# An attention block whose softmax is formed on turned scores: maximum from k's high part, exponential after the turn, one scaling per pair of heads

## The chip, the cores and the metric

The kernel runs on one core of a Trainium2 chip. The metric is the device time of one execution in microseconds (us); less is better. The median of three runs of the kernel before is 2279.28 us (2278.8 to 2279.79).

## What is computed

```python
scale_shift = emb @ W_emb + b_emb                       # 8 x 2048
xn = rms_norm(x, g_norm) * (1 + scale) + shift          # x: 8 x 512 x 1024, float32
q, k, v = split(xn @ W_qkv)                             # 16 heads of 64
q, k = rms_norm(q, g_q), rms_norm(k, g_k)
attn = softmax(q @ k.T * 64 ** -0.5)                    # 512 x 512 for each head and batch
o = attn @ v
return x + o + o @ W_out
```

Everything is float32. The kernel gets that accuracy from TensorE's one-pass float32r products by splitting each operand into a high part, rounded to float32r, and a low part, the rest: a product is then high by high, high by low and low by high.

## The kernel before, in words

**Tiling.** The work goes batch by batch (8 batches of 512 tokens, 4 token tiles of 128), and within a batch by pairs of heads (8 pairs; `it` = batch * 8 + pair counts 64 of them). Each engine has a written list of steps for the first batch (HEAD), the six in the middle (BODY) and the last (TAIL). A step is named by the pair, a letter and a number: `5S2` is step S, number 2, of pair 5; pairs 8 and 9 are the first two of the next batch, which run ahead. The engines go through their lists in order, and semaphores between them hold a step until its input is there. A step that waits holds everything behind it on its engine.

**The steps of TensorE.** C: a quarter of one token tile of the product with W_qkv, 6 matmuls of 384 columns into `proj_bank` (two banks in turn); P the same for W_out. T: 4 transposes of q (T0) or k (T1) into `flip_bank`. S: scores of head n // 4 and query tile n % 4, into `score_bank` (two in turn). F: turns the probabilities of 128 keys by all 512 queries, 4 transposes of 128 x 128 into `flip_bank` (two in turn, shared by T, F and X, which turns x). W: the product of v with the turned probabilities, two matmuls of 512 columns (high and low part of the probabilities) into `pv_bank`.

**The steps beside it.** For a projected tile: ScalarE's D copies v and squares q and k, VectorE's D sums the squares, GpSimd's D adds epsilon and raises to the power of -1/2, VectorE's M scales q and k and so frees the bank. T: ScalarE writes the high parts, VectorE the low parts. `q_split[head]` holds q's high part in the head's 64 rows and its low part in the other 64; `k_hi[head]` holds k's high part twice, so one matmul over 128 contraction rows gives (q high + q low) by k high; `k_lo[head]` has k's low part in the head's rows and zeros in the others.

For a score tile: VectorE's S takes the row maximum (negated) from PSUM; ScalarE's S takes the exponential with that as bias into `probs` and accumulates the row sum; VectorE's N takes the reciprocal of the row sum and scales the tile in place. After F: ScalarE's F copies the turned tile, rounded, to `pt_hi`, VectorE's F subtracts that from the turned tile in PSUM into `pt_lo`. O joins the two halves of `pv_bank` (ScalarE moves one to the other rows, VectorE adds), Q splits the result into `o_hi` (ScalarE) and `o_lo` (GpSimd). V splits v, L and Y split weights and x, R adds the residual, A and X normalize the next batch's x. SyncE issues the DMAs for weights, x, residual and results.

The lines concerned: TensorE's S is lines 585 to 592, F 593 to 600, W 601 to 611; ScalarE's S 714 to 720, F 721 to 724; VectorE's S 857 to 860, N 861 to 866, F 867 to 870, O 871 to 877; GpSimd's D 968 to 974.

Of the kernel before, what the change touches and what calls it, by code (L numbers as in the profile page):

```python
# [36 lines left out]
        1C5 1C6 1C7 1C8 1C9 0S0 0S1 1C10 1C11 0S2 0S3 1C12 1C13 0S4 0S5 1C14 0F0 0F1 1C15 0S6 0S7 2C0 0F2 0F3 0W0 0W1  # L37
        2C1 2C2 0W2 2C3 0W3 1T0 1T1 2C4 2C5 2C6 2C7 0F4 2C8 2C9 0F5 1S0 0F6 0W4 1S1 2C10 0F7 0W5 1S2 1S3 0W6 2C11 0W7
        2C12 1S4 1S5 1F0 1F1 2C13 2C14 1F2 1W0 1F3 1W1 1S6 1S7 1W2 2C15 1W3 3C0 3C1 1F4 1F5 3C2 3C3 2T0 2T1 1W4 1W5 3C4
        3C5 3C6 1F6 3C7 3C8 1F7 1W6 2S0 2S1 3C9 3C10 1W7 2S2 3C11 3C12 2S3 2S4 3C13 3C14 3C15 2S5 2S6 4C0 2F0 2F1 4C1  # L40
        4C2 2S7 4C3 3T0 3T1 2W0 2W1 4C4 4C5 2F2 4C6 4C7 4C8 2F3 2W2 3S0 2F4 3S1 2F5 2W3 4C9 3S2 2F6 2W4 3S3 2F7 2W5 4C10
        2W6 4C11 2W7 3S4 3S5 4C12 3F0 3F1 4C13 3S6 4C14 3F2 3W0 3F3 3W1 3S7 4C15 3W2 5C0 3W3 3F4 3F5 5C1 5C2 3F6 3F7 3W4
        3W5 5C3 5C4 4T0 4T1 3W6 3W7 5C5 5C6 5C7 5C8 5C9 4S0 4S1 5C10 5C11 4S2 4S3 5C12 5C13 4S4 4S5 5C14 4F0 4F1 5C15
        4S6 4S7 6C0 4F2 4F3 4W0 4W1 6C1 6C2 5T0 4W2 5T1 4W3 6C3 6C4 6C5 4F4 6C6 6C7 6C8 4F5 5S0 4F6 4W4 5S1 6C9 4F7 4W5
        4W6 5S2 6C10 4W7 5S3 6C11 5S4 6C12 5S5 5F0 5F1 6C13 6C14 5F2 5W0 5F3 5W1 5S6 5S7 5W2 6C15 5W3 7C0 7C1 5F4 5F5
        7C2 7C3 +X0 5W4 5W5 7C4 6T0 7C5 6T1 7C6 7C7 7C8 7C9 5F6 7C10 7C11 +X1 5W6 6S0 6S1 5F7 7C12 7C13 7C14 7C15 +X2
        5W7 6S2 6S3 8C0 8C1 +X3 8C2 6S4 6S5 8C3 8C4 6S6 8C5 7T0 6S7 8C6 7T1 8C7 8C8 8C9 6F0 8C10 8C11 6F1 6F2 6W0 7S0
        7S1 6F3 6W1 6F4 6W2 8C12 7S2 6F5 6W3 7S3 6F6 6W4 8C13 6F7 6W5 7S4 6W6 8C14 8C15 6W7 7S5 7F0 7F1 7S6 9C0 9C1 7F2
# [1102 lines left out]
```

## Time and profile before

| | |
|---|---|
| median of the runs | 2279.28 us |
| the profiled execution | 2278.89 us, its span 2276.0 us |
| TensorE, matmuls | 2256.2 us busy (99%), 13392 matmuls |
| VectorE | 1597.9 us (70%) |
| ScalarE | 1345.7 us (59%) |
| GpSimd | 651.7 us (29%) |

The span is from the first to the last instruction of the profiled execution. A matmul's end is modelled and matmuls overlap in the pipeline, so the distance between the starts of two matmuls says more than the duration of one. Durations of VectorE and ScalarE overlap slightly with their neighbours too.

### The profile page before, as it was taken

To read this page: it belongs to the slowest core of one execution; us is meant where nothing else is said; L and a number is where in the kernel's file an instruction comes from. 1 tells how busy PE (TensorE), PEld (TensorE's weight loads), DVE (VectorE), ACT (ScalarE), POOL (GpSimd) and SP (SyncE) were. 2 spreads that over 40 slices of the span, in tenths; PEclk is the share of its full clock that TensorE was granted. 3 is DMA by queue.
4 is the path that set the end of the run, shared out by engine and by line. 5 is a ranking of instruction groups with operands and counts; after the bars stand their busy time and mean duration, and the time that the engine had idled before them with its cause. 6 is when DMAs were issued, how large, how long until landed. Compare 5 with 4: busy or idle time off the path is not lost.

```text
span 2276.0 us, 36733 instructions
## 1 busy us (share of the span) xinstructions
PE 2256.2 (99%) x13392; PEld 2110.3 (93%) x13392; DVE 1597.9 (70%) x3284; ACT 1345.7 (59%) x3101; POOL 651.7 (29%) x880
## 2 busy tenths in 40 slices
PE   8999999999999999999999999999999999999999
PEld 4999989999999999999999999999999999999999
DVE  4898784787827778287872878738786487854875
ACT  4687772667616676176762667526674366743663
POOL 3444431324213241122312234122331223302220
PEclk9999999999999999999999999999999999999999
DMA  9544346422364332733236332362323723246331
GB/s 359 224 167 177 112 154 228 178 99 110 118 220 184 107 115 88 256 148 112 111 114 256 112 112 112 122 253 107 112 112 130 291 92 118 82 151 246 111 121 65
DMA packets 71269, 346.35 MB, mean 152 GB/s; under 512 B 7601, under 2 KB 43441, under 8 KB 47537
## 3 DMA queue, kind: packets, MB, share of 16 engines
q1 hardware_dynamic: 71088, 344.01, 41.2%
q8 instruction: 106, 1.74, 0.3%
q14 instruction: 75, 0.61, 0.1%
HBM read 293.65 MB, written 50.33 MB: 151 GB/s over the span
## 4 chain that ended last, share of the span: by engine, by line
PE 86%; DVE 8%; ACT 2%; issue 1%; POOL 0%; DMA 0%; ACTq 0%; DVEq 0%
PE proj_bank L502 18%; PE proj_bank L500 18%; PE proj_bank L501 18%; PE flip_bank L598 9%; PE pv_bank L609 5%; PE pv_bank L610 5%; PE score_bank L590 4%; PE score_bank L591 4%; PE flip_bank L553 2%; DVE probs L865 2%; DVE neg_max L859 2%; DVE pt_lo L869 2%; PE flip_bank L563 1%; ACT k_hi L700 1%; PE proj_bank L525 1%
## 5 line engine op out<-in xcount | busy, mean ns | idle before, releaser
L500 PE MATMUL proj_bank<-w_split,xn_hi 128*128 128x384 f32 x2048 | 700.0, 342 | 1.4 <-DVE res L907 0.8
L502 PE MATMUL proj_bank<-w_split,xn_lo 128*128 128x384 f32 x2048 | 688.5, 336 | 0.0
L501 PE MATMUL proj_bank<-w_split,xn_hi 128*128 128x384 f32 x2048 | 687.4, 336 | 0.0
L718 ACT ACTIVATE probs<-score_bank,neg_max 128x512 f32<-128x512 f32 x512 | 352.6, 691 | 213.5 <-DVE neg_max L859 211.2
L500 PEld LDWEIGHTS proj_bank<-w_split,xn_hi 128*128 128x128 f32 x2048 | 385.2, 188 | 18.1 <-DVE xn_lo L854 1.0
L501 PEld LDWEIGHTS proj_bank<-w_split,xn_hi 128*128 128x128 f32 x2048 | 385.5, 188 | 15.2
L724 ACT CAST pt_hi<-flip_bank 128x512 fp32r<-128x512 f32 x512 | 288.8, 591 | 182.0 <-PE flip_bank L598 91.1
L869 DVE TENSOR_TENSOR pt_lo<-flip_bank,pt_hi 128x512 fp32r<-128x512 f32 x512 | 339.9, 685 | 78.1 <-ACT pt_hi L724 75.9
L502 PEld LDWEIGHTS proj_bank<-w_split,xn_lo 128*128 128x128 f32 x2048 | 384.8, 188 | 0.0
L859 DVE TENSOR_REDUCE neg_max<-score_bank 128x1 f32<-128x512 f32 x512 | 341.3, 684 | 17.0 <-PE score_bank L591 13.0
L865 DVE TENSOR_SCALAR probs<-probs,row_inv 128x512 f32<-128x512 f32 x512 | 275.7, 539 | 18.1
L598 PE MATMUL flip_bank<-ident,probs 128*128 128x128 f32 x2048 | 284.4, 273 | 1.1 <-DVE q_split L830 0.4
L598 PEld LDWEIGHTS flip_bank<-ident,probs 128*128 128x128 f32 x2048 | 242.5, 140 | 32.8 <-DVE pt_lo L869 7.3
L973 POOL TENSOR_TENSOR qk_rstd<-qk_ms_eps,neg_half 128x4 f32<-128x4 f32 x256 | 264.6, 1033 | 20.0
L970 POOL TENSOR_TENSOR qk_ms_eps<-qk_ms,eps_col 128x4 f32<-128x4 f32 x256 | 55.3, 216 | 719.2 <-DVE qk_ms L880 719.1
L609 PE MATMUL pv_bank<-pt_hi,v_split 128*128 128x512 f32 x512 | 224.3, 438 | 4.2 <-DVE pt_lo L869 4.2
L500 PE MATMUL proj_bank<-w_split,o_hi 128*128 128x384 f32 (+1 forms) x672 | 215.2, 320 | 0.0
L951 POOL TENSOR_TENSOR v_split<-v_stage,v_split 128x256 fp32r<-128x256 f32 x128 | 98.9, 773 | 401.3 <-ACT v_split L688 401.3
L502 PE MATMUL proj_bank<-w_split,o_lo 128*128 128x384 f32 (+1 forms) x672 | 213.6, 318 | 0.0
L501 PE MATMUL proj_bank<-w_split,o_hi 128*128 128x384 f32 (+1 forms) x672 | 213.5, 318 | 0.0
L590 PE MATMUL score_bank<-k_hi,q_split 128*128 128x512 f32 x512 | 206.0, 402 | 0.1
L591 PE MATMUL score_bank<-k_lo,q_split 128*128 128x512 f32 x512 | 201.6, 394 | 0.0
(86 smaller groups left out, 3205.1 us busy)
## 6 DMA issues: line engine op xcount, KB each, us to landing
w_split<-w_store SPq DMA_DIRECT2D x140, 1536.0 KB, 7.0
w_store<-w_split SPq DMA_DIRECT2D x20, 1536.0 KB, 10.1
x_tile<-in_x SPq DMA_DIRECT2D x32, 512.0 KB, 11.0
w_raw<-in_w_qkv SPq DMA_DIRECT2D x16, 768.0 KB, 8.4
w_split<-w_store SPq DMA_DIRECT2D x12, 1024.0 KB, 5.1
w_raw<-in_x SPq DMA_DIRECT2D x56, 192.0 KB, 6.7
out<-w_raw SPq DMA_DIRECT2D x56, 192.0 KB, 1.9
emb_stage<-in_w_emb SPq DMA_DIRECT2D x5, 1024.0 KB, 10.6
```

The lines of the kernel that those rows point to most:

```text
L500: nc.tensor.matmul(dst, a_hi, w_hi, start=(kt == 0), stop=False)
L501: nc.tensor.matmul(dst, a_hi, w_lo, start=False, stop=False)
L502: mm = nc.tensor.matmul(dst, a_lo, w_hi, start=False, stop=(kt == KT - 1))
L590: nc.tensor.matmul(score_bank[n % 2][:, :], q_t, k_hi[h][:, :], start=True, stop=False)
L591: nc.tensor.matmul(score_bank[n % 2][:, :], q_t, k_lo[h][:, :], start=False, stop=True).then_inc(score_full, 1)
L598: mm = nc.tensor.transpose(flip_bank[flip][:, qt * P:(qt + 1) * P], probs[h][:, qt, i * P:(i + 1) * P], ident[:, :])
L609: nc.tensor.matmul(pv_bank[h][:, :], v_t, pt_hi[n % 2][:, :], start=(i == 0), stop=False)
L718: nc.scalar.activation(probs[h][:, i, :], score_bank[n % 2][:, :], ACT.Exp, bias=neg_max[:, n:n + 1], accum_out=row_sum[:, n:n + 1]).then_ ...
L724: nc.scalar.copy(pt_hi[n % 2][:, :], flip_bank[flip][:, :]).then_inc(flip_hi, 1)
L859: nc.vector.tensor_reduce(neg_max[:, n:n + 1], score_bank[n % 2][:, :], AX.X, ALU.max, negate=True).then_inc(max_done, 1)
L865: nc.vector.tensor_scalar(probs[h][:, i, :], probs[h][:, i, :], row_inv[:, n:n + 1], None, ALU.mult).then_inc(probs_ready, 1)
L869: nc.vector.tensor_tensor(pt_lo[n % 2][:, :], flip_bank[flip][:, :], f32(pt_hi[n % 2][:, :]), ALU.subtract).then_inc(flip_free, 1)
```

## The change

Step S of TensorE is one matmul, with `k_hi` alone, and serves for the maximum only. Step H (new) turns the four columns of negated maxima of a head into four rows of 128; VectorE's H lays them, by a product with the identity, as four rows of 512 over a copy of q (`q_max`, made by VectorE's Z) where `k_lo` has four rows of ones. Step F then forms the scores a second time, already turned, in two matmuls of 512 columns: `k_hi` by `q_split`, and `k_lo` by `q_max`, whose four extra contraction rows add the negated maximum. ScalarE's F takes the exponential of the turned scores into `probs`; its new step E copies that, rounded, to `pt_hi`; VectorE's F takes `pt_lo` from `probs` and `pt_hi`, both in SBUF. The probabilities stay unscaled. Their sums over the keys are formed by GpSimd's new step U (six adds of 128 x 512 a pair), ScalarE's U and VectorE's N (the two heads brought into one tile), J (high and low part) and TensorE's G, two matmuls with a matrix of ones per head. VectorE's G takes the reciprocal of the 128 x 512 sums and scales `o_pair` once. The flip banks are handed back by two semaphores, one for each engine that frees them. `o_part` and one of the three first residual buffers go. The orders of all engines but SyncE are written anew; shown are the lines of BODY that hold the steps of pair 5's scores (TensorE before; TensorE, VectorE and GpSimd after).

```diff
-        4C4 3T0 3T1 2W2 2W3 4C5 4C6 4C7 2F4 4C8 4C9 2F5 3S0 2F6 2W4 3S1 4C10 2F7 2W5 3S2 3S3 2W6 4C11 2W7 4C12 3S4 3S5
-        5C7 5C8 3F7 3W6 4S0 4S1 5C9 3W7 5C10 4S2 4S3 5C11 5C12 4S4 5C13 4S5 5C14 4F0 4F1 4S6 4S7 5C15 4F2 4F3 4W0 4W1
...
+        4H1 5C14 4W0 4F3 4F4 4W1 5C15 4F5 4F6 4W2 4W3 4F7 6C0 6C1 4W4 4W5 5T0 5T1 6C2 4W6 4W7 6C3 6C4 6C5 5S0 5S1 6C6
+        6C7 6C8 4G0 5S2 6C9 5S3 6C10 6C11 5H0 5S4 5S5 6C12 5F0 5F1 5S6 5S7 6C13 5F2 5F3 6C14 5H1 5W0 5W1 6C15 5F4 5F5
...
+        4N0 4N1 4O1 6M0 4J0 6D1 5S0 5S1 4G0 6M1 5S2 5S3 5H0 6D2 5S4 5S5 6M2 5S6 5S7 5F0 5F1 5H1 5F2 5F3 6D3 5F4 5F5 6M3
...
+        3U0 3U1 4D3 3U2 3U3 3U4 3U5 5D0 4V0 4V1 5D1 3Q0 5D2 4U0 4U1 5D3 4U2 4U3 5V0 4U4 4U5 6D0 5V1 6D1 4Q0 6D2 5U0 5U1
...
-        q_split = [sb(f"q_split{h}", [P, T], F32R) for h in range(2)]
+        q_split = sb("q_split", [P, 2, T], F32R)
+        q_max = sb("q_max", [P, 2, T], F32R)
...
-                        pe.wait_ge(exp_done, it * 8 + (n - 2 + 1 + CREDIT))
+                        wait_past(pe, max_done, it * 8 + (n - 1))
                         if n == 0:
-                            pe.wait_ge(flip_free, flip_at(order, b, "T", 1, p)[0] + 1)
-                        q_t = q_split[h][:, i * P:(i + 1) * P]
-                        nc.tensor.matmul(score_bank[n % 2][:, :], q_t, k_hi[h][:, :], start=True, stop=False)
-                        nc.tensor.matmul(score_bank[n % 2][:, :], q_t, k_lo[h][:, :], start=False,
-                                         stop=True).then_inc(score_full, 1)
+                            pe.wait_ge(qk_hi_done, it * 2 + 2)
+                            freed(pe, "T", 0, it)
+                        nc.tensor.matmul(score_bank[n % 2][:, :], q_split[:, h, i * P:(i + 1) * P], k_hi[h][:, :],
+                                         start=True, stop=True).then_inc(score_full, 1)
+                    elif kind == "H":
+                        flip_wait(pe, u)
+                        pe.wait_ge(max_done, it * 8 + 4 * n + 4)
+                        nc.tensor.transpose(flip_bank[flip][0:TT, 0:P], neg_max[:, 4 * n:4 * n + 4],
+                                            ident[:, :]).then_inc(flip_full, 1)
                     elif kind == "F":
-                        wait_past(pe, flip_free, releases(order, u))
+                        flip_wait(pe, u)
                         if i == 0:
-                            pe.wait_ge(probs_ready, it * 8 + (4 * h + 4))
-                        for qt in range(TT):
-                            mm = nc.tensor.transpose(flip_bank[flip][:, qt * P:(qt + 1) * P],
-                                                     probs[h][:, qt, i * P:(i + 1) * P], ident[:, :])
-                        mm.then_inc(flip_full, 1)
+                            freed(pe, "H", h, it)
+                            freed(pe, "T", 1, it)
+                        nc.tensor.matmul(flip_bank[flip][:, :], k_hi[h][:, i * P:(i + 1) * P], q_split[:, h, :],
+                                         start=True, stop=False)
+                        nc.tensor.matmul(flip_bank[flip][:, :], k_lo[h][:, i * P:(i + 1) * P], q_max[:, h, :],
+                                         start=False, stop=True).then_inc(flip_full, 1)
...
+                    elif kind == "G":
+                        flip_wait(pe, u)
+                        if is_first(it):
+                            pe.wait_ge(ones_ready, 2)
+                        pe.wait_ge(sum_lo_done, it + 1)
+                        nc.tensor.matmul(flip_bank[flip][:, :], head_ones[:, :], sum_hi, start=True, stop=False)
+                        nc.tensor.matmul(flip_bank[flip][:, :], head_ones[:, :], sum_lo, start=False,
+                                         stop=True).then_inc(flip_full, 1)
...
-                    elif kind == "S":
-                        act.wait_ge(max_done, it * 8 + (n + 1))
-                        if i == 0 and not (is_first(b) and p == 0):
-                            act.wait_ge(flip_full, flip_at(order, b, "F", 4 * h + 3, p - 1)[0] + 1)
-                        nc.scalar.activation(probs[h][:, i, :], score_bank[n % 2][:, :], ACT.Exp,
-                                             bias=neg_max[:, n:n + 1],
-                                             accum_out=row_sum[:, n:n + 1]).then_inc(exp_done, 1)
                     elif kind == "F":
                         act.wait_ge(flip_full, u + 1)
+                        if i == 0 and not is_first(it):
+                            if h == 0:
+                                act.wait_ge(key_sum_done, it * 2 - 1)
+                            else:
+                                freed(act, "G", 0, it - 1)
+                        nc.scalar.activation(probs[h][:, i, :], flip_bank[flip][:, :],
+                                             ACT.Exp).then_inc(flip_freed["ScalarE"], 1)
+                    elif kind == "E":
                         act.wait_ge(pv_used, it * 8 + (n - 1 + CREDIT))
-                        nc.scalar.copy(pt_hi[n % 2][:, :], flip_bank[flip][:, :]).then_inc(flip_hi, 1)
+                        owner, done = RELEASES[flip_of("F", n, it)]
+                        act.wait_ge(flip_freed[owner], done)
+                        nc.scalar.copy(pt_hi[n % 2][:, :], probs[h][:, i, :]).then_inc(p_hi_done, 1)
+                    elif kind == "U":
+                        mine, other = rows(n), rows(1 - n)
+                        act.wait_ge(keys_added, it * 6 + (5 if n == 0 else 6))
+                        nc.scalar.copy(key_moved[mine, :], probs[n][other, 3, :]).then_inc(keys_moved, 1)
+                    elif kind == "J":
+                        act.wait_ge(key_sum_done, it * 2 + 2)
+                        nc.scalar.copy(sum_hi, key_sum).then_inc(sum_hi_done, 1)
...
+                    elif kind == "Z":
+                        freed(dve, "T", 0, it)
+                        nc.vector.tensor_copy(q_max[:, :, :], f32(q_split[:, :, :])).then_inc(q_copied, 1)
...
+                    elif kind == "H":
+                        dve.wait_ge(flip_full, u + 1)
+                        dve.wait_ge(q_copied, it + 1)
+                        at = (1 - n) * DH
+                        nc.vector.tensor_tensor(q_max[at:at + TT, n, :].rearrange("p (t q) -> p t q", q=P),
+                                                flip_bank[flip][0:TT, 0:P].unsqueeze(1).to_broadcast([TT, TT, P]),
+                                                ident[0:TT, 0:TT].unsqueeze(2).to_broadcast([TT, TT, P]),
+                                                ALU.mult).then_inc(flip_freed["VectorE"], 1)
+                    elif kind == "F":
+                        dve.wait_ge(p_hi_done, it * 8 + (n + 1))
+                        nc.vector.tensor_tensor(pt_lo[n % 2][:, :], probs[h][:, i, :], f32(pt_hi[n % 2][:, :]),
+                                                ALU.subtract).then_inc(p_lo_done, 1)
                     elif kind == "N":
-                        dve.wait_ge(exp_done, it * 8 + (n + 1 + CREDIT))
-                        nc.vector.reciprocal(row_inv[:, n:n + 1], row_sum[:, n:n + 1]).then_inc(inv_done, 1)
-                        dve.wait_ge(inv_done, it * 8 + (n + 1))
-                        nc.vector.tensor_scalar(probs[h][:, i, :], probs[h][:, i, :], row_inv[:, n:n + 1], None,
-                                                ALU.mult).then_inc(probs_ready, 1)
-                    elif kind == "F":
-                        dve.wait_ge(flip_hi, u_hi + 1)
-                        nc.vector.tensor_tensor(pt_lo[n % 2][:, :], flip_bank[flip][:, :],
-                                                f32(pt_hi[n % 2][:, :]), ALU.subtract).then_inc(flip_free, 1)
+                        mine = rows(n)
+                        dve.wait_ge(keys_moved, it * 2 + (n + 1))
+                        nc.vector.tensor_tensor(key_sum[mine, :], probs[n][mine, 3, :], key_moved[mine, :],
+                                                ALU.add).then_inc(key_sum_done, 1)
+                    elif kind == "J":
+                        dve.wait_ge(sum_hi_done, it + 1)
+                        nc.vector.tensor_tensor(sum_lo, key_sum, f32(sum_hi), ALU.subtract).then_inc(sum_lo_done, 1)
+                    elif kind == "G":
+                        dve.wait_ge(flip_full, u + 1)
+                        dve.wait_ge(sum_lo_done, it + 1)
+                        dve.wait_ge(o_sum_done, it * 2 + (2 + CREDIT))
+                        nc.vector.reciprocal(sum_inv, flip_bank[flip][:, :]).then_inc(inv_done, 1)
+                        dve.wait_ge(inv_done, it + 1)
+                        nc.vector.tensor_tensor(o_pair[:, :], o_pair[:, :], sum_inv,
+                                                ALU.mult).then_inc(flip_freed["VectorE"], 1)
                     elif kind == "O":
                         dve.wait_ge(o_part_done, it * 2 + (n + 1))
-                        if n == 0:
-                            dve.wait_ge(o_lo_done, it + 1)
                         mine = rows(n)
-                        nc.vector.tensor_tensor(o_pair[mine, :], pv_bank[n][mine, :], o_part[mine, :],
+                        nc.vector.tensor_tensor(o_pair[mine, :], pv_bank[n][mine, :], o_pair[mine, :],
                                                 ALU.add).then_inc(o_sum_done, 1)
...
+            def add_keys(it, n):
+
+                head, part = n // 3, n % 3
+                e = probs[head]
+                if part < 2:
+                    pool.wait_ge(p_lo_done, it * 8 + (4 * head + 2 * part + 2))
+                    src, dst = 2 * part, 2 * part + 1
+                else:
+                    pool.wait_ge(keys_added, it * 6 + n)
+                    src, dst = 1, 3
+                op = nc.gpsimd.tensor_tensor(e[:, dst, :], e[:, src, :], e[:, dst, :], ALU.add)
+                op.then_inc(keys_added, 1)
 
```

## Rows read from the trace of the kernel before

**Rows 1.** The page, parts 1 and 2: busy time, and the granted clock by slices.

```profile
PE 2256.2 (99%) x13392; PEld 2110.3 (93%) x13392; DVE 1597.9 (70%) x3284; ACT 1345.7 (59%) x3101; POOL 651.7 (29%) x880
...
PEclk9999999999999999999999999999999999999999
```

**Rows 2.** The page, part 4: the chain that ended last, by engine.

```profile
PE 86%; DVE 8%; ACT 2%; issue 1%; POOL 0%; DMA 0%; ACTq 0%; DVEq 0%
```

**Rows 3.** The waits: who waited for whom, us in total, times, longest.

```profile
PE pv_bank L609 <- DVE pt_lo L869: 4.2, 7, 0.6
```

**Rows 4.** The timeline of TensorE: start, duration, line, operands, count.

```profile
700.28 0.40 PE L590 MATMUL score_bank<-k_hi,q_split 128*128 128x512 f32 x1
700.52 0.39 PE L591 MATMUL score_bank<-k_lo,q_split 128*128 128x512 f32 x1
700.74 0.34 PE L500 MATMUL proj_bank<-w_split,xn_hi 128*128 128x384 f32 x1
...
701.79 1.03 PE L598 MATMUL flip_bank<-ident,probs 128*128 128x128 f32 x8
702.58 0.42 PE L500 MATMUL proj_bank<-w_split,xn_hi 128*128 128x384 f32 x1
702.84 0.34 PE L501 MATMUL proj_bank<-w_split,xn_hi 128*128 128x384 f32 x1
```

**Rows 5.** Groups of TensorE by line and form: busy, mean ns, idle before.

```profile
L598 PE MATMUL flip_bank<-ident,probs 128*128 128x128 f32 x2048 | 284.4, 273 | 1.1 <-DVE q_split L830 0.4
```

**Rows 6.** The same view for VectorE.

```profile
L859 DVE TENSOR_REDUCE neg_max<-score_bank 128x1 f32<-128x512 f32 x512 | 341.3, 684 | 17.0 <-PE score_bank L591 13.0
L869 DVE TENSOR_TENSOR pt_lo<-flip_bank,pt_hi 128x512 fp32r<-128x512 f32 x512 | 339.9, 685 | 78.1 <-ACT pt_hi L724 75.9
L865 DVE TENSOR_SCALAR probs<-probs,row_inv 128x512 f32<-128x512 f32 x512 | 275.7, 539 | 18.1
...
L880 DVE TENSOR_REDUCE qk_ms<-sq 128x4 f32<-128x256 f32 x256 | 106.1, 414 | 86.2 <-ACT sq L742 83.6
...
L863 DVE RECIPROCAL row_inv<-row_sum 128x1 f32<-128x1 f32 x512 | 80.7, 158 | 55.1 <-ACT probs L718 54.0
...
L918 DVE TENSOR_SCALAR gq_col<-gq_raw 128x1 f32<-128x1 f32 x1 | 0.1, 147 | 0.0
```

**Rows 7.** The same view for ScalarE.

```profile
L718 ACT ACTIVATE probs<-score_bank,neg_max 128x512 f32<-128x512 f32 x512 | 352.6, 691 | 213.5 <-DVE neg_max L859 211.2
L724 ACT CAST pt_hi<-flip_bank 128x512 fp32r<-128x512 f32 x512 | 288.8, 591 | 182.0 <-PE flip_bank L598 91.1 <-PE pv_bank L610 88.6
...
L718 ACT ACTIVATION_READ_ACCUMULATOR probs<-score_bank,neg_max 128x1 f32 x512 | 102.3, 200 | 0.0
L742 ACT ACTIVATE sq<-proj_bank 128x256 f32<-128x256 f32 x256 | 100.5, 393 | 0.0
```

**Rows 8.** The same view for GpSimd.

```profile
L973 POOL TENSOR_TENSOR qk_rstd<-qk_ms_eps,neg_half 128x4 f32<-128x4 f32 x256 | 264.6, 1033 | 20.0
...
L966 POOL TENSOR_TENSOR o_lo<-o_pair,o_hi 128x512 fp32r<-128x512 f32 x64 | 84.3, 1317 | 381.1 <-ACT o_hi L734 380.9
```

**Rows 9.** The timeline of VectorE in the first batch.

```profile
40.78 0.69 DVE L854 TENSOR_TENSOR xn_lo<-y_half,xn_hi 128x512 fp32r<-128x512 f32 x1 [0.30 <-ACT xn_hi L666]
...
42.85 3.79 DVE L767 TENSOR_TENSOR w_split<-w_raw,w_split 128x384 fp32r<-128x384 f32 x3
...
49.72 0.55 DVE L767 TENSOR_TENSOR w_split<-w_raw,w_split 128x384 fp32r<-128x384 f32 x1
```

**Rows 10.** The timeline of GpSimd in the same stretch.

```profile
42.64 2.29 POOL L933 TENSOR_TENSOR w_split<-w_raw,w_split 128x384 fp32r<-128x384 f32 x2
```

**Rows 11.** The timeline of all engines around 297 us.

```profile
297.56 1.57 POOL L966 TENSOR_TENSOR o_lo<-o_pair,o_hi 128x512 fp32r<-128x512 f32 x1
...
298.65 0.66 PE L553 MATMUL flip_bank<-ident,qk_stage 128*128 128x128 f32 x4 [1.48 <-DVE pt_lo L869]
```

**Rows 12.** Busy time of each engine in a dense stretch: us, count, clock, DMA.

```profile
850.00:900.00 50.00, 49.91 (x294) 46.25 (x293) 41.70 (x83) 33.82 (x76) 11.44 (x16) 1.00 0.30 110
```

More of the change, by code:

```diff
@@ L226, in flip_buf, with order_of, flip_table @@
-def flip_buf(order, kind, n, p):
-    places = HEAD_FLIPS if order is HEAD else TAIL_FLIPS if order is TAIL else BODY_FLIPS
-    before = 0 if order is HEAD else HEAD_FLIPS[1]
-    assert BODY_FLIPS[1] % 2 == 0
-    return (before + places[0][(kind, n, p)][0]) % 2
-FIRST_X = {HEAD_FLIPS[0][("X", r, 0)][0] for r in range(TT)}
-def releases(order, u):
-    return u if order is HEAD and u - 2 in FIRST_X else u - 1
+def order_of(b):
+    return HEAD if b == 0 else TAIL if b == B - 1 else BODY
+def flip_table():
+    table, releases, counts = {}, [], {"ScalarE": 0, "VectorE": 0}
+    for b in range(B):
+        for step in order_of(b)["TensorE"]:
+            p, d, kind, n = read_step(step)
+            if kind in "TFXHG":
+                table[(kind, n, b + d if kind == "X" else b * PAIRS + p)] = len(releases)
+                for owner in ("VectorE", "ScalarE") if kind == "X" else ("ScalarE",) if kind == "F" else ("VectorE",):
+                    counts[owner] += 1
+                    releases.append((owner, counts[owner]))
+    return table, releases
@@ L337, in cond_attention @@
         v_split = [sb(f"v_split{h}", [P, TT, P], F32R) for h in range(2)]
-        probs = [sb(f"probs{h}", [P, TT, T]) for h in range(2)]
+        probs = [sb("probs0", [P, TT, T])]
+        with nc.sbuf_tensor("sum_split", [P, TT, T], F32R) as sum_split:
+            pass
+        probs.append(sb("probs1", [P, TT, T]))
         pt_hi = [sb(f"pt_hi{i}", [P, T], F32R) for i in range(2)]
@@ L557, in cycle @@
                         for half in range(2):
-                            wait_past(pe, flip_free, releases(order, u + half))
+                            flip_wait(pe, u + half)
                             if half == 0:
@@ L911, in _ @@
             for head in range(2):
-                nc.vector.memset(f32(k_lo[head][rows(1 - head), :]), 0.0)
+                op = nc.vector.memset(f32(k_lo[head][rows(1 - head), :]), 0.0)
+            op.then_inc(k_lo_zero, 1)
+            dve.wait_ge(k_lo_zero, 1)
+            for head in range(2):
+                nc.vector.memset(f32(k_lo[head][(1 - head) * DH:(1 - head) * DH + TT, :]), 1.0)
             for kt in range(0, KT, 2):
```

383 lines of the change are left out of this document (198 added, 185 removed).

## The prediction

> **What bounds the kernel now.** I read the page first: TensorE is busy for 2256.2 of 2276.0 us and its granted clock stands at nine tenths or more in all forty slices, the upper level of 2.4 GHz [rows 1]. Busy ends are modelled, so I went to the chain of waits: 86% of it is TensorE, 8% VectorE [rows 2], and the table of waits, where the largest wait of a matmul in the attention is 4.2 us in all [rows 3]. Then the timeline of TensorE alone, for its true prices, which are the distances between starts: 0.46 us for two matmuls of 512 columns (0.230 each, against 0.40 of "duration"), 1.05 us for one C step of six matmuls of 384 columns, and 0.79 us for 8 transposes after which the next matmul comes 0.26 instead of 0.17 us later, so 0.875 per 8, 0.109 each [rows 4]. The reader should see there that nothing waits: every matmul starts when the one before it has been fed. So the time is TensorE's list of instructions, plus some waits. The steps of its three orders, counted from the code and priced so, sum to 2201 us; the other 75 us of the span (the start before the first batch, and small waits) I leave as they are. In a dense stretch VectorE is busy for 41.7 of 50 us, 83% [rows 12]: the next bound is near.
>
> **TensorE, the terms.** There are 64 pairs (8 batches by 8), 8 tiles each.
> - F loses its transposes: 2048 of them [rows 5] by 0.109 = 224.0 us.
> - S loses its second matmul: 512 by 0.230 = 117.8 us.
> - F gains two matmuls of 512 columns: 1024 by 0.230 = 235.5 us.
> - G: 2 matmuls by 64 by 0.230 = 29.4 us.
> - H: 2 single transposes a pair. The trace has none alone; 0.055 (half of one, since only 4 weight columns are loaded) and 0.2 (one plus the later start of the next matmul) bound it. I take 0.109, the row's mean: 14.0 us, ends 7 and 26.
> Net: 224.0 + 117.8 - 235.5 - 29.4 - 14.0 = 62.9 us less, all of it on the path, since TensorE is it. By H's ends, 51 to 70.
>
> **What now has to hide.** ScalarE: the exponential stays (691 ns, now from the turned scores and without bias), its 8 reads of the accumulator (200 ns) go, the copy to pt_hi stays at about its 591 ns [rows 7]; U twice and J once are three such copies, 1.8 us for 1.6 us gone. Neutral, at 60% busy. One wait gets shorter: a score bank is free after the maximum alone, and a flip bank after the exponential alone.
> VectorE, by a pair: gone are 8 scalings at 539 ns and 8 reciprocals at 158, 5.6 us. New are Z (1024 columns, between 0.66 and 1.4; by the scaling's 539 for 512, about 1.0), H twice, N twice, J and G's product, six instructions at about 685 each [rows 6], 4.1 us, and G's reciprocal of 512 columns. By the slope of the row reductions, 684 against 414 ns for 256 columns more [rows 6], VectorE goes at 1.05 ns an element, so 0.69. Sum 5.8: no change, if two things hold, and both become rivals below.
> GpSimd: U, 6 adds of 512 columns a pair, at o_lo's 1317 ns [rows 8]: 7.9 us a pair, 506 us in all, on top of 652. It isn't full (52%), but its queue also holds D, whose power takes 1033 ns and ends in the release of a projection bank. The order has D behind one or two U steps (4U0 4U1 5D3), so M3 comes up to 1.3 us later; four C steps (4.2 us) stand between two uses of a bank, against a chain of 0.3 + 0.4 + 0.4 + 0.2 + 1.0 + 0.4 = 2.7 us, so 1.3 us fits but not 2.6.
>
> **The walk where it is tightest.** In BODY, TensorE from the end of 5S1: 6C6 6C7 6C8 (3.15), 4G0 (0.46), 5S2 (0.23), 6C9 (1.05), 5S3 (0.23), 6C10 6C11 (2.10): 5H0 is reached at 7.22 us. VectorE has 6D1 before 5S0, and 6D1's tile ends with 6C7 at 2.10; ScalarE's copy and square take some 0.66 (the square 393 ns [rows 7], the copy of half as many columns 0.27 by estimate), 6D1 ends at 3.2, then 5S0 5S1 4G0 6M1 5S2 5S3 at 0.68 + 0.68 + 1.38 + 0.42 + 0.68 + 0.68: 7.7 by durations, some 7.2 if each starts 0.1 us before its forerunner's end, as rows in sequence do. So 5H0 has no slack, and everything dearer on VectorE between 5S0 and 5H0 is a wait of TensorE, once a pair. In the same way 5H0 to 5F0 is 1.5 us, against about 1.0 for VectorE's H and its semaphores: fits. From F to its W stand 3.3 to 6.4 us, against 0.69 + 0.6 + 0.69 and some 0.3 for the semaphores = 2.3: at least 1.0 to spare. W7 to the next G is 5.7 us or more; O, N, J lie in it.
>
> **The shared port.** The rows of VectorE with two inputs from SBUF: 0.55 us for 384 columns and 0.69 for 512 alone, but three of 384 columns in 3.79 us, 1.26 each [rows 9], while GpSimd ran two of its own in 2.29 us [rows 10]. And it has reached TensorE once: around 297 us GpSimd's o_lo took 1.57 instead of 1.32, and a transpose waited for VectorE's pt_lo, 1.48 us idle [rows 11]. Before, pt_lo took one input from PSUM and never met this (685 mean, [rows 6]); now all 8 pt_lo a pair have both in SBUF, as have N, J and G's product, and GpSimd's SBUF work grows from about 3 to 11 us a pair, some 0.4 of a dense pair's 27 us. An instruction that arrives in a GpSimd add waits for 0.65 on the mean: 12 by 0.4 by 0.65 = 3 us of VectorE's time a pair. Most of it falls in the F stretch, where ScalarE's 1.3 us for each F sets the pace and the 1.0 us above covers it. I take 0.4 us a pair as what gets through to TensorE, 25 us; the ends are 0 and 3 us a pair.
> The Trainium skill, SBUF — State Buffer, Who interferes with whom, says that a VectorE instruction with two SBUF inputs contends with a GpSimd instruction that reads SBUF, and that the later one waits for the whole of the earlier; [rows 9, 10] agree (1.26 against 0.55). By that rule the worst single wait is one add, 1.3 us.
>
> **Sum.** From the profiled execution (span 2276.0, whole time 2278.9, which is 0.4 under the median of the three runs): 2278.9 - 62.9 + 25 = 2241 us. Its own range: 2208 (no new wait, H at its low end) to 2265.
>
> **Rival A, the reciprocal becomes the wait (slower).** The trace has the reciprocal of one column only: 158 ns against 147 for a scaling of one column [rows 6]. Those 11 ns bound it from above at 1 + 11, or 12 ns an element, 6 us for 512; from below it is 0.69. If the divider takes 8 turns an element at 1.05 ns, G's reciprocal is 512 by 8.4 = 4.3 us, 3.6 more than I put in, and by the walk nearly all of it becomes a wait of TensorE before H0, in some 60 of 64 pairs: 3.3 by 60 = 200 us, so 2440. Half of that speed gives 2330. It decides from 1.0 us a pair over my price, a reciprocal of 1.7 us. For it: only the one-column row. Against it: the reductions, at two lengths, go at 1.05 ns an element, and 11 ns lie within the spread of such short rows. I put 0.17 on it.
> The Trainium skill, VectorE: DVE Perf Modes, First, the fixed hardware budget, says the reciprocal is an iterative divide with a repeat count of 8; that speaks for this rival, and no row here can show its rate over many columns.
>
> **Rival B, the port eats the gain.** If 1 us of the 3 a pair reaches TensorE, because pt_lo, then M and the next S slip together: 64 us, so 2280; at 0.6 us a pair 2254, at 1.5 it is 2312. It decides from 0.98 us a pair. For it: VectorE at 83% in a dense stretch [rows 12] plus 3 us a pair is some 95% of 27 us, and the 1.48 us of [rows 11]. Against: the slack of F to W. Chance 0.17, for 2265 to 2310.
>
> **Chances and range.** Forecast 0.66, A 0.17, B 0.17. A measurement of this kernel can't tell less than about 0.2%, 4.6 us, from nothing. Faster by more: the forecast and half of B, 0.75. Within: 0.04 of B. Slower: A and the rest of B, 0.21. Range 2208 to 2305: that leaves out A and a little at either end.
>
> **What would show it.** Right: TensorE's F groups as two matmuls 0.23 apart; a batch's period near 272 us instead of 278; pt_lo's mean between 0.8 and 1.0 us with single ones at 1.9; U at 1.3 us; waits of TensorE for VectorE's maximum or H under 1 us a pair. Wrong: a RECIPROCAL of 512 columns above 1.7 us with H or S waiting for a maximum behind it (A); VectorE above 90% in the dense stretches and W waiting for pt_lo (B); an F matmul further apart than 0.23 us, which would break the first sum.

## The result, and the profile after

| | median of the runs | ratio to before, 95% |
|---|---|---|
| before | 2279.04 us (2277.61 to 2279.79) | 1 |
| after | 2539.49 us (2537.11 to 2543.43) | 1.1145 (1.1126 to 1.1165) |

The change makes the kernel 260 us slower; forecast was 2241 us, 38 us faster, and the range ended at 2305. The page of the changed kernel, part 1 (span 2539.1 us), answers to [rows 1]:

```profile
PE 2312.5 (91%) x12112; PEld 2057.5 (81%) x12112; DVE 1942.9 (77%) x2777; ACT 1379.0 (54%) x2781; POOL 1227.3 (48%) x1264
```

TensorE has 1280 matmuls fewer, as the change says, and is no longer busy all the time: 91% instead of 99%. VectorE, which was to have the same work, has 345 us more. The groups of VectorE and GpSimd, in the columns of [rows 6, 8], say where:

```profile
L932 DVE RECIPROCAL probs<-flip_bank 128x512 f32<-128x512 f32 x64 | 214.4, 3350 | 1.4 <-PE flip_bank L635 0.4
L918 DVE TENSOR_TENSOR pt_lo<-probs,pt_hi 128x512 fp32r<-128x512 f32 x512 | 421.1, 851 | 134.8 <-ACT pt_hi L754 133.0
L923 DVE TENSOR_TENSOR probs<-probs 64x512 f32<-64x512 f32 x128 | 103.1, 805 | 11.0 <-ACT probs L758 7.8
L1020 POOL TENSOR_TENSOR probs<-probs 128x512 f32<-128x512 f32 x384 | 513.9, 1342 | 424.6 <-DVE pt_lo L918 418.3
```

The first row is G's reciprocal: 3350 ns, not 0.69 us, 170 us more than priced over 64 pairs. pt_lo's mean rose from 685 ns [rows 6] to 851, as expected; U, the last row, takes the 1.3 us of [rows 8]. L923 is N. Z takes 1271 ns (L882) and J 771 (L927). The waits, as in [rows 3] (who waited for whom, us in total, times, longest):

```profile
PE score_bank L602 <- DVE neg_max L906: 45.9, 32, 2.4
PE proj_bank L512 <- DVE qk_stage L949: 39.2, 32, 2.7
PE flip_bank L607 <- DVE neg_max L906: 36.3, 23, 2.5
PE pv_bank L626 <- DVE pt_lo L918: 20.3, 43, 3.5
PE flip_bank L614 <- DVE o_pair L934: 17.8, 11, 2.2
```

Before, the largest of this kind was 4.2 us in all [rows 3]. Now S (L602), H (L607), C (L512) and F (L614) wait for something that VectorE delivers behind the reciprocal; W's wait (L626) is no shorter without it (22.1 us in experiment 1). One such place, near the end, where the rest is quiet; VectorE first, then TensorE (start, duration, line, tiles, count, idle before it and the releaser):

```profile
2487.71 3.35 DVE L932 RECIPROCAL probs<-flip_bank 128x512 f32<-128x512 f32 x1
2491.09 0.69 DVE L934 TENSOR_TENSOR o_pair<-o_pair,probs 128x512 f32<-128x512 f32 x1
2491.70 1.28 DVE L906 TENSOR_REDUCE neg_max<-score_bank 128x1 f32<-128x512 f32 x2
```

```profile
2492.44 0.79 PE L602 MATMUL score_bank<-k_hi,q_split 128*128 128x512 f32 x1 [2.30 <-DVE neg_max L906]
...
2493.35 0.52 PE L538 MATMUL proj_bank<-w_split,o_hi 128*128 128x384 f32 x1
2493.67 0.52 PE L539 MATMUL proj_bank<-w_split,o_lo 128*128 128x384 f32 x1
```

The maximum that frees a score bank stands in VectorE's queue behind 3.35 + 0.69 us, and TensorE stands idle for 2.3 us. The reader should also see what comes behind the wait: P's matmuls start 0.32 us apart instead of 0.175, up to 2494.95. The same stretch by windows (columns after the length: busy us and count of PE, PEld, DVE, ACT, POOL, then the granted clock):

```profile
2490.00:2492.00 2.00, 0.14 (x1) 0.00 (x0) 1.97 (x3) 0.18 (x1) 0.00 (x0) 1.00 0.00 0
2492.00:2495.00 3.00, 2.56 (x8) 2.27 (x9) 2.04 (x4) 0.43 (x1) 1.28 (x1) 0.55 0.00 0
```

After the wait the clock is granted at 0.55, nearly the lower level of 1.2 GHz. Its mean over the span is 0.976 against 0.999 before. Were TensorE busy in all of the time at the lower level, it would have lost 0.024 by 2539 = 61 us there; that is the most it can be.

A dense stretch, in the columns of [rows 12], has VectorE at 95%:

```profile
1250.00:1300.00 50.00, 41.20 (x207) 35.11 (x207) 47.26 (x65) 28.38 (x58) 28.21 (x28) 1.00 0.20 71
```

It is the fullest 50 us of the trace. Nine of its 50 such stretches stand at 90% or more; before it was 1 of 45.

### The profile page after: what moved, and what is told of

It is laid out like the page before. It is cut to its first block and busy times, and to the rows that moved or that the text cites. A ratio compares the mean times of both kernels' runs of the same rounds, so it can differ in the third digit from the quotient of the medians.

```text
span 2539.1 us, 34110 instructions
## 1 busy us (share of the span) xinstructions
PE 2312.5 (91%) x12112; PEld 2057.5 (81%) x12112; DVE 1942.9 (77%) x2777; ACT 1379.0 (54%) x2781; POOL 1227.3 (48%) x1264
## 3 DMA queue, kind: packets, MB, share of 16 engines
q8 instruction: 97, 1.59, 0.3%
## 5 line engine op out<-in xcount | busy, mean ns | idle before, releaser
L512 PE MATMUL proj_bank<-w_split,xn_hi 128*128 128x384 f32 x2048 | 714.4, 349 | 40.0 <-DVE qk_stage L949 39.2
L1020 POOL TENSOR_TENSOR probs<-probs 128x512 f32<-128x512 f32 x384 | 513.9, 1342 | 424.6 <-DVE pt_lo L918 418.3
L513 PE MATMUL proj_bank<-w_split,xn_hi 128*128 128x384 f32 x2048 | 701.9, 343 | 0.0
L918 DVE TENSOR_TENSOR pt_lo<-probs,pt_hi 128x512 fp32r<-128x512 f32 x512 | 421.1, 851 | 134.8 <-ACT pt_hi L754 133.0
L512 PEld LDWEIGHTS proj_bank<-w_split,xn_hi 128*128 128x128 f32 x2048 | 395.2, 193 | 74.1 <-DVE qk_stage L949 52.6
L748 ACT ACTIVATE probs<-flip_bank 128x512 f32<-128x512 f32 x512 | 288.8, 603 | 195.4 <-PE flip_bank L616 189.3
L754 ACT CAST pt_hi<-probs 128x512 fp32r<-128x512 f32 x512 | 299.1, 625 | 89.2 <-PE pv_bank L627 86.7
L1052 POOL TENSOR_TENSOR qk_ms_eps<-qk_ms,eps_col 128x4 f32<-128x4 f32 x256 | 82.1, 321 | 407.0 <-DVE qk_ms L943 407.0
L771 ACT CAST o_hi<-o_pair 128x512 fp32r<-128x512 f32 x64 | 39.6, 619 | 398.3 <-DVE o_pair L934 250.2
L614 PE MATMUL flip_bank<-q_split,k_hi 128*128 128x512 f32 x512 | 209.9, 410 | 46.8 <-DVE o_pair L934 17.8
L602 PE MATMUL score_bank<-k_hi,q_split 128*128 128x512 f32 x512 | 203.8, 441 | 47.2 <-DVE neg_max L906 45.9
L1048 POOL TENSOR_TENSOR o_lo<-o_pair,o_hi 128x512 fp32r<-128x512 f32 x64 | 87.6, 1368 | 325.9 <-ACT o_hi L771 325.9
L626 PE MATMUL pv_bank<-pt_hi,v_split 128*128 128x512 f32 x512 | 213.2, 416 | 21.1 <-DVE pt_lo L918 20.3
L512 PE MATMUL proj_bank<-w_split,o_hi 128*128 128x384 f32 (+1 forms) x672 | 217.4, 323 | 5.3 <-DVE res L970 4.3
L932 DVE RECIPROCAL probs<-flip_bank 128x512 f32<-128x512 f32 x64 | 214.4, 3350 | 1.4 <-PE flip_bank L635 0.4
```

Source lines behind the costliest of these rows:

```text
L512: nc.tensor.matmul(dst, a_hi, w_hi, start=(kt == 0), stop=False)
L513: nc.tensor.matmul(dst, a_hi, w_lo, start=False, stop=False)
L614: nc.tensor.matmul(flip_bank[flip][:, :], k_hi[h][:, i * P:(i + 1) * P], q_split[:, h, :], start=True, stop=False)
L626: nc.tensor.matmul(pv_bank[h][:, :], v_t, pt_hi[n % 2][:, :], start=(i == 0), stop=False)
L748: nc.scalar.activation(probs[h][:, i, :], flip_bank[flip][:, :], ACT.Exp).then_inc(flip_freed["ScalarE"], 1)
L754: nc.scalar.copy(pt_hi[n % 2][:, :], probs[h][:, i, :]).then_inc(p_hi_done, 1)
```

## The experiments

All times are medians; "a pair" is a 64th of the difference. VectorE's busy time is that of part 1 of each page: 1597.9 us before, 1942.9 after. The runs of the kernel before beside them gave 2277.7 to 2278.9 us.

**1. e1_copy: the division taken out of the change.**

```diff
-nc.vector.reciprocal(sum_inv, flip_bank[flip][:, :]).then_inc(inv_done, 1)
+nc.vector.tensor_copy(sum_inv, flip_bank[flip][:, :]).then_inc(inv_done, 1)
```

> The changed kernel with G's reciprocal of 128 x 512 replaced by a plain copy of the same shape (left out: the division, so o is scaled by the sums). Theory R, the reciprocal is the cause: VectorE is 3.35 - 0.6 = 2.7 us a pair shorter, nearly all of it waits of TensorE (64 x 2.7 = 173 us), and most of the 33 stretches at the lower clock go with it: 2300 to 2340 us. Theory P, the shared port is the cause: at most 40 us less, 2500 us.

Measured: 2357.94 us, ratio 1.0348 (1.0332 to 1.0363). 181.5 us less than after, 2.84 a pair, for 2.67 us of VectorE (3350 - 681 ns). S's wait nearly goes, and H's falls to 1.4 us in all:

```profile
PE score_bank L602 <- DVE neg_max L906: 7.7, 9, 1.3
```

The clock went from 0.976 to 0.991, which is up to 40 of those us. So the reciprocal is 70% of the loss, and 79 us of it are something else. With them the time lies 18 us above the range expected.

**2. e2_no_port: GpSimd's adds on 8 columns instead of 512** (most of the sums over the keys is left out).

```diff
-op = nc.gpsimd.tensor_tensor(e[:, dst, :], e[:, src, :], e[:, dst, :], ALU.add)
+op = nc.gpsimd.tensor_tensor(e[:, dst, 0:8], e[:, src, 0:8], e[:, dst, 0:8], ALU.add)
```

> The changed kernel with GpSimd's six adds a pair cut from 512 to 8 columns (left out: most of the sum over the keys). The reciprocal stays. It takes GpSimd's port time away and with it the waits of pt_lo (851 against a median of 692 ns). Theory R: 512 x 0.16 = 82 us of VectorE's time, a part of it on TensorE: 2470 to 2510 us. Theory P: 2330 us or less.

Measured: 2497.57 us, 1.0954 (1.0936 to 1.0973): 42 us less, 0.65 a pair. pt_lo's mean fell from 851 to 727 ns and Z's from 1271 to 698; VectorE is busy for 123 us less (1820.2), a third of which comes through.

**3. e3_both: both edits.**

> Both edits together (left out: the division and most of the sum over keys). Whatever is left over the 2216 us of the span before less 62.9 is neither the reciprocal nor the port. R and P both: 2235 to 2260 us, clock near 1.0. If it stays above 2300, a third cause exists, such as GpSimd's later D or the new chain S, H, F.

Measured: 2292.19 us, 1.0055 (1.004 to 1.007). With the division out of the way the adds cost 2358 - 2292 = 66 us, 1.03 a pair, more than beside it. VectorE is busy for 136 us less than in e1 (1653.0 against 1789.0), 2.1 a pair. The victims of the adds aren't pt_lo alone. Z, with one input from SBUF, is one; e1 first, then e3:

```profile
L882 DVE CAST q_max<-q_split 128x1024 fp32r<-128x1024 f32 x64 | 81.3, 1270 | 1.7
```

```profile
L882 DVE CAST q_max<-q_split 128x1024 fp32r<-128x1024 f32 x64 | 44.7, 698 | 1.7
```

What is left is 32 us over the expected range and still not faster than before: there is a third loss.

**4. e4_half: half of the columns by reciprocal, half by copy.**

```diff
+nc.vector.reciprocal(probs[1][:, 1, 0:256], flip_bank[flip][:, 0:256])
+nc.vector.tensor_copy(probs[1][:, 1, 256:512], flip_bank[flip][:, 256:512]).then_inc(inv_done, 1)
```

> The changed kernel with the reciprocal of 256 columns and a copy of the other 256 (left out: half of the division). VectorE's part is 1.7 + 0.35 us instead of 3.35. If each us of it costs TensorE a us, the time is halfway between the changed kernel and the copy: 2430 us for R. If slack takes up the first microsecond it is nearer to the copy: 2390.

Measured: 2417.98 us (two executions), 1.0609, clock 0.998 and 0.994. The two take 1.75 + 0.36 us:

```profile
L932 DVE RECIPROCAL probs<-flip_bank 128x256 f32<-128x256 f32 x64 | 111.9, 1748 | 1.4 <-PE flip_bank L635 0.4
```

The first 1.42 us of VectorE cost 60 us (0.66 each), the next 1.24 cost 122 (1.5 each). The second half costs more than its own time; it is there that the clock falls, to 0.976. It doesn't simply follow VectorE's load: e1, with less of it, stands at 0.991.

**5. w2_lnexp: a whole version, the reciprocal on ScalarE as exp(-ln x).**

```diff
+nc.scalar.activation(sum_inv, flip_bank[flip][:, :], ACT.Ln).then_inc(ln_done, 1)
+nc.scalar.activation(sum_inv, sum_inv, ACT.Exp, scale=-1.0).then_inc(flip_freed["ScalarE"], 1)
```

> A version meant to be whole: the reciprocal as exp(-ln(sum)) on ScalarE, at the place just before Q or the next F in its order; VectorE's G is the product alone. ScalarE gets 1.2 us and two table loads of 1.28 us a pair. Theory R: as the copy kernel less 0.6 us of VectorE and plus ScalarE's delays before F0's exponential, up to 1 us a pair: 2310 to 2370 us. Theory P: 2500 us.

Measured: 2505.83 us, 1.0996 (1.0975 to 1.1016). A miss: only 34 us of the 181. Each of the two functions loads a table each time (L755 for Ln; L757, for Exp, has a row with the same 64 loads of 1283 ns), and VectorE's product, which kept its place in the order, waits for ScalarE instead:

```profile
L755 ACT ACT_TABLE_LOAD x64 | 82.1, 1283 | 1.1
```

```profile
DVE o_pair L939 <- ACT probs L757: 188.8, 57, 6.0
```

The work left VectorE, the wait stayed in its queue.

**6. e7_memset: e1 with GpSimd kept as busy, but reading nothing** (the division and the sums are left out). Port or queue?

```diff
-op = nc.gpsimd.tensor_tensor(e[:, dst, :], e[:, src, :], e[:, dst, :], ALU.add)
+nc.gpsimd.memset(e[:, src, :], 1.0)
+op = nc.gpsimd.memset(e[:, dst, :], 1.0)
```

> Leaves out: G's division (a copy in its place) and the sums over the keys (GpSimd writes ones, two memsets of 512 columns for each U step, which read nothing from SBUF). Question: e3's gain over e1 (2358 to 2292) came from GpSimd's adds shrinking. Was it the shared port that they held, or the time that they took in GpSimd's queue ahead of the power that frees a projection bank? The two memsets keep the queue about as busy and hold no input from SBUF. Theory, the port: 2285 to 2305, VectorE's pt_lo at 0.73 us mean as in e3 and no pt_lo above 1.0 us. Rival, the queue: 2345 to 2365, pt_lo as short, but waits of C for qk_stage (POOL power late) as in e1. If memset proves much shorter than 0.6 us each the queue is only partly loaded and a fast run tells little; the duration is to be read first.

Measured: 2298.95 us, 1.0092 (1.0077 to 1.0107). The two memsets take 1.05 us together, against 1.34 for the add, pt_lo's mean is 727 ns (729 in e3) and VectorE is busy for 1662.0 us. So of the 66 us 59 come from what GpSimd's adds read, the shared port, and 7 from its queue, with 78% of the add's time kept in it. One sign did not come: some pt_lo still take over 1.0 us, the longest 1803 ns, beside GpSimd's other work (xn_lo, o_lo).

**7. e10_load_elsewhere: e1 and 2.46 us of reciprocals a pair at another place**, behind the pt_lo of tile 7; their output goes nowhere.

> e1 (G's division left out, 2358) with seven extra reciprocals of 32 columns on VectorE in each pair, behind the pt_lo of tile 7, where W has over 1 us to spare; at 6.5 ns an element and some 0.1 us between them about 2.5 us of VectorE a pair. Output of these goes nowhere. Theory A, only the place counts (the walk from 5S0 to 5H0): this place has slack, at most 0.5 us a pair gets through, 2358 to 2390. Theory B, the load counts (VectorE was at 90% of the dense stretches already, so any 2.5 us is paid wherever it stands): 2358 plus 1.3 to 2.5 us by 64, so 2440 to 2520.

Measured: 2449.96 us, 1.0757 (1.0741 to 1.0773): 92 us, 1.44 a pair for seven of these:

```profile
L925 DVE RECIPROCAL scratch<-neg_half 128x32 f32<-128x32 f32 x448 | 157.4, 351 | 13.2
```

That is 58% of the 2.46 us put in. But VectorE's busy time grew by 97 us only (1886.5 against 1789.0), 1.52 a pair: the added work also moved Z and N away from GpSimd's adds (Z takes 738 ns instead of 1270, N 703 instead of 811). Of what VectorE had more to do, 94% is paid. I had expected at most 0.5 us a pair to get through: theory A, as it was put, falls. The run doesn't exclude that there is some spare time, since 2.46 less the 1.0 of the walk is 1.46 as well; place and load aren't told apart by it.

**8. e5_before_load: the kernel before with 2.76 us of reciprocals a pair**, nothing of it left out.

> The kernel before, all its work kept, with five extra reciprocals of 64 columns on VectorE in each pair right after the scaling of tile 0 (a stretch where the next maxima wait behind them); their output goes nowhere. At 6.5 ns an element some 2.6 us a pair. Question: is the price of a long reciprocal a matter of this change's orders, or does the kernel before pay the same? Theory, any kernel here with VectorE at 83% pays most of it: before plus 1.3 to 2.5 us by 64, 2360 to 2440. Rival, the kernel before has the room (its VectorE waits are all short and it has 17% left): under 0.5 us a pair, 2279 to 2310.

Measured: 2443.51 us, 1.0728 (1.071 to 1.0746). 166 us, 2.59 a pair: 94% of it is paid in the kernel before too, a little more than expected. At this place it didn't have the 17% that it seems to have in [rows 12]: the maxima stand behind the added work, which TensorE's rigid order turns into waits (its longest now: S for the exponential, 41.9 us, W for pt_lo, 39.2 us).

**9. e11_no_n: e3 with N's addition as a copy** (the sums are left out altogether).

```diff
-nc.vector.tensor_tensor(key_sum[mine, :], probs[n][mine, 3, :], key_moved[mine, :],
-                        ALU.add).then_inc(key_sum_done, 1)
+nc.vector.tensor_copy(key_sum[mine, :], probs[n][mine, 3, :]).then_inc(key_sum_done, 1)
```

> e3 (division and GpSimd's wide adds left out, 2292) with N's addition of two SBUF tiles replaced by a copy of one of them, so the sum of the keys is left out altogether. Theory: in e3 N still holds the shared port against GpSimd's power (1.45 instead of 1.01 us), which frees a projection bank late, so C waits 1.3 us once a batch and some smaller times: those waits go, 5 to 12 us less, 2280 to 2287, the longest power at 1.01. Rival: the power is late for another reason (its place in VectorE's and GpSimd's orders), 2289 to 2293.

Measured: 2266.48 us, 0.9951 (0.9936 to 0.9966). The expected 5 to 12 us were too few: 25.7 us, for 2 by 0.25 = 0.49 us of VectorE a pair. The wait that I had named does shrink, but not more than by 8 us; e3 first, then e11:

```profile
PE proj_bank L512 <- DVE qk_stage L949: 14.3, 25, 2.0
```

```profile
PE proj_bank L512 <- DVE qk_stage L948: 5.9, 10, 1.6
```

And GpSimd's longest power is still 1460 ns, where I had said 1.01 us. In e3 the longest stand beside N, in e11 beside pt_lo, which has two inputs from SBUF as well; those above 1.1 us fell from 45 to 21. So that mechanism explains a part at most. VectorE is busy for 30 us less (1623.0), and 86% of that is gained, near to the shares of experiments 7 and 8.

**10. w4_eight_columns: a whole version with a reciprocal of 8 columns.** The core (R is a new step of TensorE; N, J and ScalarE's U are gone):

```diff
+for part in range(2 * TT):                          # G: row sums as 128x8
+    mm = nc.tensor.matmul(flip_bank[flip][:, part:part + 1],
+                          probs[part % 2][:, 3, part // 2 * P:(part // 2 + 1) * P],
+                          ones_col[:, :], start=True, stop=True)
+nc.vector.reciprocal(inv8[:, :], flip_bank[flip][:, 0:2 * TT])
+for part in range(2 * TT):                          # R: one row of inverses per query column
+    mm = nc.tensor.matmul(flip_bank[flip][rows(part % 2), part // 2 * P:(part // 2 + 1) * P],
+                          inv8[:, part:part + 1].to_broadcast([P, DH]), ident[:, :],
+                          start=True, stop=True)
```

> A whole version, nothing left out, in which the long reciprocal isn't needed: GpSimd's sums over the tiles stay (U), but G is now eight small fp32 matmuls, each with 128 queries of the summed probabilities as stationary and one column of ones moving, so the row sums come out as 128 by 8; VectorE's reciprocal has 8 columns; a new TensorE step R (eight small matmuls of the inverses spread over 64 columns against the identity) turns them to one row per head, and the product reads them from PSUM. The two additions N, the copies U of ScalarE and J on both engines go. VectorE's load by a pair: N 1.61, J 0.77, reciprocal 3.35 gone, 6.25 by 8 and 0.15, so 0.2, back: 5.5 us less than in the changed kernel. Theory, the load of VectorE and what stands before H is the loss: it should land near e1 (2358), lower by N and J (e11 gave 26 us for 0.49 us a pair), higher by TensorE's extra: R 8 by 0.05 to 0.095 and G 8 by 0.06 to 0.3 less its old 0.46, so 25 to 170 us; forecast 2370, 2320 to 2440. Rival, the loss lies mainly in the port and the clock: above 2450, as half of the orders' waits stay.

Measured: 2428.89 us, 1.0664 (1.0646 to 1.0682): 111 us less than after, inside the range expected and 59 over its middle. The waits for VectorE's maxima have gone (H's are 1.1 us in all) and W's for pt_lo are down to 11.0; TensorE is the bound again, at 98%, with more work:

```profile
PE 2387.3 (98%) x14032; PEld 2173.3 (90%) x14032; DVE 1594.8 (66%) x2585; ACT 1263.9 (52%) x2589; POOL 1179.8 (49%) x1264
```

```profile
L935 DVE RECIPROCAL inv<-flip_bank 128x8 f32<-128x8 f32 x64 | 13.2, 206 | 82.7 <-PE flip_bank L633 82.7
```

Each of the small matmuls in the code, 8 of G and 8 of R a pair, has two records in the trace. By the distances between starts G's 1024 records take 111.6 us (0.109 each) and R's 1024 take 66.4 (0.065 each), 178 us in place of G's 30. Without these 148 us it would stand at about 2281, an estimate that takes them all to be on the path. No version of the runs that computes the whole reference beats the kernel before; e11 is faster only because it leaves work out.

## Why the prediction was wrong

**The step that failed** is the price of one instruction: "VectorE goes at 1.05 ns an element, so 0.69", the slope of the row reductions carried over to G's reciprocal. The runs give five widths: 206 ns for 8 columns, 351 for 32, 551 for 64, 1748 for 256, 3350 for 512, a line of 150 + 6.25 ns a column. The row of one column, 158 ns [rows 6], lies on it too, but one width gives no slope. I set it against a one-column scaling of 147 and got "12 ns an element at most", a factor of 2 too high; the reductions, the row of another operation, were a factor of 6 too low, and I chose by them. Rival A had the right mechanism and the right place, with a chance of 0.17; with bounds of 0.69 and 6 us and no row between them that was too little. Its point of decision is mis-summed: the 1.0 us leaves out the 25 us of the port that the forecast holds, with them it is 38 / 60 = 0.63 over the price, a reciprocal of 1.3 us. 3.35 is beyond either. For 3.35 us its own sum gives 2241 + 2.66 by 60 = 2401; the 138 us beyond are the terms below: 21 more for the reciprocal, 41 more for the port, 76 for the rest.

**TensorE's terms** held nearly. By distances between starts F's transposes came to 196.5 us (0.096 each) in the kernel before, where I had 224.0 from one group of 8; F, S and G matmuls are 0.23 apart; the next matmul starts some 0.03 us behind one of H's transposes (0.109 priced). e11 and e3 against before, with the starts' excess over their usual distance taken off (76 and 94 us, before 35), give a saving of 52 and 48 us against 62.9. With each group's median as the usual distance the same traces give up to 60, so the term was 3 to 15 us too high. The low end of its range, 2278.9 - 62.9 - 7, is 2209 and not 2208.

**The walk** named the place rightly: there the maxima come late and S and H wait. It was too strict in that each us behind 5S0 is a wait in 60 pairs: H waits in 23 places and S in 32, and the first 1.42 us cost 0.66 each (e4). That the wait moves the clock was not in it: up to 40 us between e1 and after. It also said that what is added in the stretch from F to W is covered by 1.0 us; e10 put 2.46 us a pair there and 1.44 came through, which the 1.0 would allow, but of the 1.52 us by which VectorE's busy time grew almost nothing was covered.

**The shared port** was put at 0.4 us a pair, with ends of 0 and 3: it is 1.03 without the division beside it, of which 0.1 is queue by e7, and 0.65 with it. The count behind it, 3 us of VectorE's time a pair from 12 instructions, measured 2.1 (e1 less e3). pt_lo has 1.0 of them (0.86 us on the mean with the adds, 0.73 without), N and G's product 0.3; 0.57 fall on Z, which has one input from SBUF and was not among the 12. Before, too, instructions with one such input met it: 46 of the 512 scalings of [rows 6] took over 0.6 us, up to 1.59 beside o_lo. About half of the 2.1 gets through; "most of it is covered" is what was off. Rival B's point of decision, 0.98 us a pair, is met in e1: even at my price for the reciprocal the change would have gained nothing, as e1 (ratio 1.035) shows with a copy of just that price. In [rows 11] the pt_lo that the transpose waited for took its usual 0.68 us; what came late ahead of it were two w_split of VectorE, 2.65 us beside GpSimd's w_split. That is the port too, but not by o_lo. The Trainium skill, SBUF — State Buffer, Who interferes with whom, was weighed in the prediction: the later of two such instructions waits for the whole of the earlier. The trace agrees: the longest pt_lo, 1809 ns, began 0.02 us behind an add of 1.29 us and ended 0.54 us after it.

**What I had at nothing.** "Sum 5.8: no change" for VectorE doesn't hold even with the reciprocal at 0.69: it is busy for 55 us more than before in e3, without the wide adds, and for 191 us more in e1, with them. N and J were priced at 685 and take 805 and 771 ns; Z was priced at 1.0 us and takes 1.27, or 0.70 out of the adds' way. e11 shows that 0.49 us of N a pair is worth 26 us. That VectorE has room at 83% is refuted by e5 for the place that it tried.

The balance: before 2279; TensorE's shorter list -50 (by the first count above); VectorE's longer list and the waits of the new orders +63 (this gives e3, 2292); the adds +66 (e1, 2358), 59 of them the port; the reciprocal +181 (after, 2539). The adds and the reciprocal are differences of runs. The +63 is a remainder, larger if the -50 is, of which only N's 26 is shown. C's waits for a projection bank, which the prediction took to fit, are in it (0.2 us in all before, 14.3 in e3, 5.9 in e11); what makes up the rest of the other 37 us stays open.

## What to carry to other kernels

Price an operation by rows of that same operation, and where only bounds are there let the far end have its share of the chance: a reciprocal of 512 columns here costs five copies. Don't take the idle share of an engine beside a full one, in a rigid order, for room. Where instructions were added, lengthened or cut on VectorE, its busy time changed by 30, 73, 97, 154 and 162 us (e11, e4, e10, after, e5), and 86, 82, 94, 118 and 102% of that showed in the time; the 118% has the clock in it. Where only its waiting for the port went (123 and 136 us, e2 and e3), 34 and 48% did. So compare an engine's busy time between two runs, and not the length of what was put in: work that moves also changes what it collides with. To move an expensive operation, move its wait too, or shrink its data first.

## What the runs showed of the hardware

- A reciprocal on VectorE takes 150 + 6.25 ns a column (fp32, 8 to 512 columns), a copy of 512 columns 681 ns. The Trainium skill, VectorE: DVE Perf Modes, First, the fixed hardware budget, gives the reciprocal a repeat count of 8; the measured 6.25 ns is 6 times the 1.05 ns that the reductions took, so the direction agrees and the size is nearer to 6.
- TensorE's clock stood at 0.55 for the 3 us behind a wait of 2.3 us; P's matmuls were then 0.32 us apart instead of 0.175. That wait cost more than its length.
- GpSimd's add held VectorE's subtraction (0.69 alone, 1.81 at the longest) and also a copy with one input from SBUF (Z, 0.69 alone, 1.72 at the longest); beside two memsets of GpSimd in the add's place (e7) their means are 0.73 and 0.70. GpSimd's small power (128x4) took 1.45 us instead of 1.01 when N or pt_lo, with two inputs from SBUF, ran beside it.
- A matmul of fp32 in the code has two records in the trace. With one moving column and 128 by 128 weights it costs 0.22 us, with 64 weight columns and 128 moving 0.13; a transpose with 4 weight columns 0.03 (distances between starts).
- Ln after Exp and Exp after Ln each loaded a table, 1283 ns each time, 128 times.
